# Attention scores in quarter-array matmuls, one stacking transfer for queries and keys, maxima rows from SyncE, and another start, middle and end

## What is computed

```
# attention, 16 heads of width 8
q, k, v = LN(x) @ Wq.T + bq, ctx @ Wk.T + bk, ctx @ Wv.T + bv
x = x + softmax(q k.T / sqrt(8)) v @ Wo.T + bo
# FFN with two gates (so, si) over the 128 channels of every token
x2 = LN(x)
gate = softmax(GELU(BatchNorm(conv(x2))) @ lin_w.T + lin_b)      # BatchNorm over all 8192 tokens
out  = (x2 @ W) * top32(gate_so) + (x2 * top32(gate_si)) @ W + bias
x = x + out
```

## Time and profile before

| | |
|---|---|
| median of 3 runs | 560.53 us (558.9 to 560.83) |
| the profiled execution | 563.33 us |
| its span, first to last instruction | 560.8 us, so 2.5 us lie around it |
| mean granted TensorE clock | 0.737 of full speed |
| busy share | PE 72%, DVE 79%, ACT 67%, POOL 59% |
| stage 1, step t=0 starts | 34.6 us |
| stage 1 ends, stage 2 starts | about 303 us, 311 us |

### The profile page before, as it was taken

The page is one execution under the profiler, slowest core; times in us unless marked ns, Lnnn a source line. Parts: engine busy times, 40 slices in busy tenths (PEclk is TensorE's granted clock), DMA queues, the critical chain, the costliest instruction groups (busy, mean ns, idle before and its releaser), DMA issues.

```text
span 560.8 us, 15570 instructions
## 1 busy us (share of the span) xinstructions
PE 405.9 (72%) x5186; PEld 316.1 (56%) x5186; DVE 440.5 (79%) x2165; ACT 375.1 (67%) x1060; POOL 330.2 (59%) x402
## 2 busy tenths in 40 slices
PE   3467988999998999988992766666666666666432
PEld 1135766777777777777860545545555555445331
DVE  7745666777877777776541799999999999999990
ACT  2425676877788777766655967777677666676652
POOL 6466676887677777562112046666666666666666
PEclk9857999999999999999795555555555555555555
DMA  4888786888887887675000000000000000000000
GB/s 135 177 206 207 193 199 151 194 185 185 192 195 191 206 187 185 161 168 123 4 4 1 0 2 19 19 20 20 19 20 19 20 20 19 20 20 19 19 20 19
DMA packets 138680, 52.78 MB, mean 94 GB/s; under 512 B 105115, under 2 KB 130908, under 8 KB 137052
## 3 DMA queue, kind: packets, MB, share of 16 engines
q1 hardware_dynamic: 136424, 51.27, 37.8%
q10 hardware_dynamic: 2176, 0.52, 0.4%
HBM read 34.47 MB, written 16.78 MB: 91 GB/s over the span
## 4 chain that ended last, share of the span: by engine, by line
DVE 41%; SPq 33%; DMA 9%; PE 7%; issue 5%; POOL 2%; ACT 2%; POOLq 0%; ACTq 0%; DVEq 0%
SPq L273 30%; DVE kst L868 22%; DVE top_next L859 12%; DMA k_scratch<-k_parts 6%; DVE top_first L859 4%; DMA qst<-q_scratch 3%; SPq L258 3%; PE ps_pv L329 1%; PE ps_col L314 1%; POOL kst L963 1%; ACT x2n L550 1%; PE ps_mix L534 1%; PE ps_row L358 1%; PE ps_row L503 1%; SPq L220 1%
## 5 line engine op out<-in xcount | busy, mean ns | idle before, releaser
L738 DVE TENSOR_REDUCE m<-ps_row 128x8 f32<-128x512 f32 x128 | 82.4, 686 | 54.5 <-PE ps_row L358 54.2
L868 DVE MATCH_REPLACE8 kst<-top_next,kst 128x128 f32<-128x128 f32 x384 | 101.2, 282 | 0.0
L545 ACT ACTIVATE pT<-ps_col 128x512 f32<-128x512 f32 x128 | 68.7, 589 | 37.1 <-PE ps_col L314 37.1
L859 DVE MAX8 top_next<-kst 128x8 f32<-128x128 f32 x384 | 78.2, 282 | 0.0
L329 PE MATMUL ps_pv<-vx,pT 128*64 128x18 f32 x2048 | 72.5, 213 | 0.0
L329 PEld LDWEIGHTS ps_pv<-vx,pT 128*64 128x64 f32 x2048 | 66.1, 139 | 6.3 <-issue 4.2
L519 PE MATMUL ps_proj<-wf_sb,x2T 128*128 128x128 f32 x128 | 33.2, 441 | 45.8 <-ACT x2T L682 45.8
L519 PEld LDWEIGHTS ps_proj<-wf_sb,x2T 128*128 128x128 f32 x128 | 28.5, 328 | 52.2 <-ACT x2T L682 52.2
L550 ACT ACTIVATE x2n<-xr,nm,rs 128x128 f32<-128x128 f32 x128 | 52.6, 493 | 4.2 <-POOL nm L888 4.2
L959 POOL TENSOR_SCALAR neg_max<-top_first 128x4 f32<-128x4 f32 x32 | 7.1, 222 | 74.8 <-DVE top_first L859 74.8
L358 PE MATMUL ps_row<-kst,qst 96*64 96x128 bf16 x1024 | 42.3, 226 | 12.1 <-DMA qst<-q_scratch 12.0
(11 more groups left out here) (103 smaller groups left out, 1092.7 us busy)
## 6 DMA issues: line engine op xcount, KB each, us to landing
k_scratch<-k_parts SPq DMA_DIRECT2D x32, 192.0 KB, 3.1
q_scratch<-q_parts SPq DMA_DIRECT2D x32, 192.0 KB, 3.0
kst<-k_scratch SPq DMA_DIRECT2D x32, 192.0 KB
qst<-q_scratch SPq DMA_DIRECT2D x32, 192.0 KB
xr<-in_x_dram SPq DMA_DIRECT2D x16, 256.0 KB, 4.3
cT<-in_ctxT_dram SPq DMA_DIRECT2D x16, 256.0 KB, 3.7
kst<-k_scratch SPq DMA_DIRECT2D x32, 128.0 KB
qst<-q_scratch SPq DMA_DIRECT2D x32, 128.0 KB
```

Source lines behind the costliest of these rows:

```text
L545: act.activation(pT[:, b % PT_RING, :, :], ps_col[b % 2][:, :, :], ACT.Exp, scale=SCALE).then_inc(act_exp, 1)
L738: dve.tensor_reduce(m32[:, b // 4, :, 4 * j:4 * j + 4].rearrange("q a h -> q h a"), ps_row[b % 2][:, :, :, :], AX.X, ALU.max).then_inc(dve ...
L859: ins = dve.max(top[:, n, :], src)
L868: ins = dve.match_replace(picked[s][:, p, cols], top[:, n, :], src, PICKED)
```

## The change

- The two sequences of a pair lie in different halves of the partitions (rows 0 to 49 and 64 to 113), with no zeros. `key_side` and `query_side` make four instructions for every head and `hp`, each 48 or 50 rows by 64 output partitions by 64 streamed columns, one in each quarter of the array. Their number doubles. Each call covers 8 heads and both `ps_row` or `ps_col` banks, so that it waits for both maxima (or exponentials) of the call before.
- PE's order: each query-side block now follows the key-side block at a quarter's start; it stood after the `values` block that closes a quarter.
- Queries and keys share a tensor `stacks`; 6 stacking transfers of both take the place of 12, and the keys' pieces are now 8 KB long, as the queries' were. The maxima rows go out from SP in two transfers per half group (`maxima`), in SP's order between the others.
- POOL starts `split_queries` only when `max_parts(t, 0)` is done.
- The start: no memsets of the stacks, weights fetched by ACT, an activation that loads ACT's table early, the first keys split by DVE, the first and last layer norms partly on DVE. The middle: batch norm coefficients mostly on DVE, GELU ahead of the repeated normalisation. The end: the last round is done gate by gate, and the last group is combined on DVE, with its transposes and products in halves over four PSUM banks.

The diff, cut to its core:

```diff
-STRIDE = 4
-MROWS = 2 * ROWS
-KROWS = MROWS + 4
+
+KROWS = ROWS + 2
...
+    start = a * 64 + {3: 0, 2: 1, 1: 1 + 2 * 2 * DH}[n]
+    return slice(start, start + 2 * (n * DH - 1) + 1, 2)
...
-        qst = [sb(f"qst{s}", [128, HEADS, HALF], BF16) for s in range(STACKS)]
-        kst = [sb(f"kst{s}", [128, HEADS, PAIRS, 2, SEQ], BF16) for s in range(STACKS)]
-        cT = [sb(f"cT{s}", [128, PAIRS, 2 * SEQ]) for s in range(CTX_RING)]
+
+        stacks = [sb(f"stacks{s}", [128, 2, HEADS, HALF], BF16) for s in range(STACKS)]
+        qst = [stacks[s][:, 0, :, :] for s in range(STACKS)]
+        kst = [stacks[s][:, 1, :, :] for s in range(STACKS)]
...
+            def stack(g):
                 s, d = g % 2, slot(g)
-                wait(sp, done[s], WRITES * (g // 2 + 1))
+                wait(sp, k_out[s], WRITES * (g // 2 + 1))
+                wait(sp, q_out[s], WRITES * (g // 2 + 1))
+
+                wait(sp, pe_col, 8 * (g - STACKS + 1))
+                for n in RUNS:
+                    for a in range(2):
+
+                        if n == 1:
+                            src = scratch[s][a, 0:2 * PARTS:2 * PARTS - 1]
+                            src = src.rearrange("k (i h) t -> i k (h t)", h=HEADS)
+                        else:
+                            step = 2 * PARTS - n
+                            src = scratch[s][a, 0:2 * step].rearrange("(k n) (i h) t -> k n i h t", k=2, h=HEADS)[:, 0:n]
+                            src = src.rearrange("k n i h t -> (n i) k (h t)")
+                        sp.dma_start(stacks[d][spread(a, n), :, :, :].rearrange("r k h t -> r k (h t)"), src).then_inc(moved[d], 16)
...
+            def maxima(g, hp):
+                wait(sp, act_mT, 2 * g + hp + 1)
+                wait(sp, pe_col, 8 * (g - STACKS + 1))
                 for a in range(2):
-                    for n in RUNS:
-                        first = PARTS - n if to_keys else 0
-                        src = scratch[s][a, first:first + n].rearrange("n (i h) t -> (n i) (h t)", h=HEADS)
-                        rows = spread(a, n)
-                        dst = (kst[d][rows, :, :, a, :].rearrange("r h p m -> r (h p) m") if to_keys
-                               else qst[d][rows, :, :].rearrange("r h t -> r (h t)"))
-                        if to_keys:
-                            src = src.rearrange("r (x m) -> r x m", m=SEQ)
-                        sp.dma_start(dst, src).then_inc(moved[d], 16)
+                    rows = slice(a * 64 + ROWS, a * 64 + KROWS)
+                    sp.dma_start(qst[slot(g)][rows, :, hp * 128:(hp + 1) * 128],
+                                 mT[a * 2 * HEADS:(a + 1) * 2 * HEADS, hp, :]).then_inc(m_moved[hp][slot(g)], 16)
...
+                if there(t - 1):
+                    maxima(t - 1, 1)
                 if there(t + 1):
-
-                    wait(sp, act_mT, 2 * t)
-                    wait(sp, pe_col, 8 * (t - 1))
-                    stack(t + 1, k_scratch, k_out, k_moved, True)
-                    stack(t + 1, q_scratch, q_out, q_moved, False)
+                    stack(t + 1)
+                if there(t):
+                    maxima(t, 0)
                 if there(t + 2):
-                    write_parts(t + 2, k_parts, k_scratch, k_out, k_moved)
-                    write_parts(t + 2, q_parts, q_scratch, q_out, q_moved)
+                    write_parts(t + 2, k_parts, PARTS, k_out)
+                    write_parts(t + 2, q_parts, 0, q_out)
...
+                wait(pe, act_exp, 8 * g + 4 * hp + 2 * j)
+                for hh in range(HEADS // 2):
+                    h = j * (HEADS // 2) + hh
+                    for pp, a in ((0, 0), (1, 1), (1, 0), (0, 1)):
+                        rows = slice(a * 64, a * 64 + KROWS)
+                        cols = slice((2 * hp + pp) * SEQ, (2 * hp + pp + 1) * SEQ)
+                        mm = pe.matmul(ps_col[a][pp * SEQ:(pp + 1) * SEQ, hh, :], kst[s][rows, h, cols], qst[s][rows, h, cols],
+                                       start=True, stop=True)
+                        if hh == HEADS // 2 - 1 and pp != a:
+
+                            mm.then_inc(pe_col, 1)
...
+            def query_side(g, hp, j):
+                s = slot(g)
+                if hp == 0 and j == 0:
+                    wait(pe, moved[s], STACK * uses(g))
+
+                wait(pe, dve_max, 8 * g + 4 * hp + 2 * j)
+                for hh in range(HEADS // 2):
+                    h = j * (HEADS // 2) + hh
+                    for pp, a in ((0, 0), (1, 1), (1, 0), (0, 1)):
+                        rows = slice(a * 64, a * 64 + ROWS)
+                        cols = slice((2 * hp + pp) * SEQ, (2 * hp + pp + 1) * SEQ)
+                        mm = pe.matmul(ps_row[a][pp * SEQ:(pp + 1) * SEQ, hh, :], qst[s][rows, h, cols], kst[s][rows, h, cols],
+                                       start=True, stop=True)
+                        if hh == HEADS // 2 - 1 and pp != a:
+
+                            mm.then_inc(pe_row, 1)
...
                 if d:
                     key_side(t - 1, 0, 0)
+                if c:
+                    query_side(t, 0, 0)
                 if e:
                     out_proj(t - 2, 0)
                 if q and t > FIRST + 1:
                     keys(t + 2)
-
                 if d:
                     turn_max(t - 1, 1)
                 if e:
                     values(t - 2, 1, 1)
+
+                if d:
+                    key_side(t - 1, 0, 1)
                 if c:
-                    query_side(t, 0)
-                    query_side(t, 1)
-
-                if d:
-                    key_side(t - 1, 0, 1)
+                    query_side(t, 0, 1)
                 if q:
                     queries(t + 2)
                 if f:
                     turn_x2(t - 3)
                 if e:
                     turn_attn(t - 2, 1)
-
                 if d:
                     values(t - 1, 0, 0)
+
+                if d:
+                    key_side(t - 1, 1, 0)
                 if c:
-                    query_side(t, 2)
-                    query_side(t, 3)
-
-                if d:
-                    key_side(t - 1, 1, 0)
+                    query_side(t, 1, 0)
                 if e:
                     out_proj(t - 2, 1)
                 if c:
                     values_in(t)
-
-                if c:
                     turn_max(t, 0)
                 if d:
                     values(t - 1, 0, 1)
-                if c:
-                    query_side(t, 4)
-                    query_side(t, 5)
                 if f:
                     convolve(t - 3)
 
                 if d:
                     key_side(t - 1, 1, 1)
+                if c:
+                    query_side(t, 1, 1)
                 if n:
                     turn_x(t + 3)
                 if d:
                     turn_attn(t - 1, 0)
-
                 if d:
                     values(t - 1, 1, 0)
-                if c:
-                    query_side(t, 6)
-                    query_side(t, 7)
...
-                wait(act, pe_col, 8 * (g - STACKS + 1))
-                wait(act, act_mT, 2 * g + hp + 1)
-                act.dma_start(qst[slot(g)][MROWS:KROWS, :, hp * 128:(hp + 1) * 128],
-                              mT[:, hp, :]).then_inc(m_moved[hp][slot(g)], 16)
...
+            for dst, src in ((wk_sb, wk), (bqk_sb, bqk), (wq_sb, wq)):
+                act.dma_start(dst[:, :], src).then_inc(qk_in, 16)
+
+            act.wait_ge(dve_half, 2)
+            act.activation(nothing[:, 1:2], nothing[:, 0:1], ACT.Identity)
...
-                j = b % 4
-                if j == 0:
-                    wait(dve, dve_m, 2 * (g - 1) + b // 4 + 1)
-                dve.tensor_reduce(m32[:, b // 4, :, 4 * j:4 * j + 4].rearrange("q a h -> q h a"), ps_row[b % 2][:, :, :, :],
+                hp, j, a = b // 4, (b // 2) % 2, b % 2
+                if b % 4 == 0:
+                    wait(dve, dve_m, 2 * (g - 1) + hp + 1)
+                dve.tensor_reduce(m32[:, hp, a, j * (HEADS // 2):(j + 1) * (HEADS // 2)], ps_row[a][:, :, :],
                                   AX.X, ALU.max).then_inc(dve_max, 1)
...
+            def urgent_rstd(g, ag, ve, rs, nm, ready, added, powered, done):
+
+                wait(dve, ready, g + 1)
+                dve.tensor_scalar(ve[:, :], ag[:, :, 1], LN_EPS, None, ALU.add).then_inc(added, 1)
+                wait(dve, powered, 4 * g + 4)
+                dve.scalar_tensor_tensor(nm, ag[:, :, 0], -1.0, rs, ALU.mult, ALU.mult).then_inc(done, 1)
...
-            dve.memset(kst[0][:, :, :, :, :].bitcast(F32).rearrange("r h p a m -> r (h p a m)"), 0.0).then_inc(dve_zero, 1)
...
+            s = (GROUPS - 1) % 2
+            inner, outer = slice(DIM, 2 * DIM), slice(0, DIM)
+            dve.wait_ge(a2_left, GROUPS)
+            dve.tensor_tensor(expd[s][:, :, inner], expd[s][:, :, inner], picked[s][:, :, inner], ALU.subtract).then_inc(d2_last, 1)
+            dve.wait_ge(d2_last, 1)
+            dve.wait_ge(a2_x2, GROUPS)
```

(16 more changed lines are left out.)

295 lines of the change are left out of this document (162 added, 133 removed).

## The result

The changed kernel takes 624.12 us (median of 4 runs, 622.6 to 625.71), the kernel before 559.71 us beside it. The ratio is 1.116, 95% interval 1.110 to 1.122. The forecast had the sign and missed the size: 575, with a range that ended at 607. Times are medians over all executions; the ratios leave out those more than 1.5% above their kernel's fastest, so the kernels of 590.54 and 603.53 us, with one execution left each (575.98 and 594.33), have none.

The account below looks back on a forecast made before the run. SP's stacking transfers bound stage 1 at 15.6 us a step, PE 1.15 us behind, and DVE bounds stage 2. New waits add 30 us, edges save 15: +15, so 575 us, range 552 to 607.

Parts of the forecast that it names:

- SP's round: SP's transfer issue per loop step: from 15.15 us to 11.5, at worst 13.8, so SP stops being the bound.
- The score pair: Key-side plus query-side block on PE: 0.9 us for 64 instructions, 1.1 with changes of form, against 1.02 before.
- The reading that explained two rows with one number: PE score and value blocks: 64-column weight loads set the time, about 58 ns each, 14.5 ns with four side by side.
- The new waits: PE waits for DVE's maxima ahead of the query side: 2.0 us in the second quarter, 1.05 in the fourth.
- The step: One stage 1 loop step: 14.8 + 2.0 + 1.05 = 17.8 us against 15.6, +30 us over 14 steps.
- only streaming counts: Rival for PE's score pairs: 0.47 + 0.2 us a pair, 16.5 us a step, 555 us in all; chance 0.25.
- The clock: Rival: PE's new waits drop its clock to 1.2 GHz, 3.4 us a stretch, 599 to 623 us, put at 605; chance 0.20.
- I cost that at nothing, up to 1 us a step: Maxima transfers on SP, first half's queued behind the stack: no cost, up to 1 us if the fourth quarter gets short.
- the end (-6): After DVE's last replace: gate-by-gate work and halved transposes and products finish near 552, saving 6 us.
- the middle (-2.3): Between the stages: renormalisation behind the first GELU and an early table load on ACT save 2.3 us.
- The start (-7): First query-side block comes at 27.5 instead of 34.61, saving 7 us (4 to 8).
- 2.7 to land: Start: time from the last query stack's issue to the first query-side block, 34.61 - 31.95 = 2.7 us, assumed unchanged.

Follow-up runs that it names:

- 590.54: Changed kernel with DVE's maxima ahead of the normalisations, maxima rows issued by ACT, and twelve stacking transfers in 8 KB packets instead of six; 590.54 us.
- 603.53 us: The 590.54 us kernel with the first half's maxima rows sent sooner, and PE's output product and keys ahead of the first key side; 603.53 us.
- the edges' kernel: The kernel before with only the changed kernel's start, middle and end, its loop, layout and transfers kept; 553.31 us, ratio 0.984.
- the quarter kernels: The changed kernel and the ten follow-ups that keep its score products in quarters of the array; 581.11 to 624.12 us.
- the split one: The kernel before with each score product issued as two of half its streamed columns, 64 instead of 32 a quarter; 570.75 us, ratio 1.022.

## Why the prediction missed, step by step

- **SP's round** (11.5, at worst 13.8) and its leaving the chain: right, with 9.7 us of issue a step and 4.34 of them for the stack instead of 5.
- **The score pair** (0.9 for 64 instructions, 1.1 in all): wrong. It takes 0.67 us. The reading that explained two rows with one number, a shared weight load of 58 ns, fell (it set float32 value products beside bf16 query-side ones); the lower bound, streaming alone, holds: 178.60 - 178.33 = 0.27 us for the 32 key-side instructions, 8 ns each. Doing without the zeros thus does give PE something, 4 x 0.35 us a step. The Trainium skill's load time by columns ("TensorE: Matmul & The Clock Gate", LDWEIGHTS), shared by four as the forecast shared it, gave an estimate of 0.85 us for the 64; the trace, with 0.27 us for 32 and 0.67 for the pair, doesn't agree, and the measurement decides.
- **The new waits** (2.0 and 1.05 us): the place, the releaser and the first size were right (1.88); the second was 0.49, with 0.34 us more spent ahead of the convolution on ACT's copy.
- **The step** (17.8): the only one of the changed kernel with the clock up throughout takes 16.6 (282.0 to 298.6). That is the 16.5 of the rival "only streaming counts", whose sizes were the right ones.
- **The clock** was a rival at 0.20, and it is what happened. This is the step that failed: the sum of the forecast priced the new wait with the clock at 2.4 GHz and had no term for its falls. I set against it that one step in sixteen had fallen before. But the idle time of 1.28 us in the earlier trace rows was itself one of few over a microsecond, and I forecast a longer one in every step. The price of a fall was about right, the number was not: 14 falls instead of seven, with stretches of 3.4 to 20 us, 8 on average, at 0.40 of each (below) make 45 us, where the rival's "in all" had 48. Falls and pauses of issue together take steps from 16.6 to 20.3 us: 14 x 3.7 = 52 us. The kernel before with the new order alone shows wait and clock together: 14 x (18.9 - 15.5) = 48 us.
- **What I had no term for:** pauses of issue, 11.2 us here and up to 29 us once the wait was gone, and maxima rows that land late. "I cost that at nothing, up to 1 us a step" was too low: with the wait gone, they took 1.5 to 3 us at a time.
- **Edges:** the end (-6) right to 0.1 us and the middle (-2.3) nearly, with 5.2 - 3.7 = 1.5 here and 1.7 in the edges' kernel. Alone, middle and end made 553.31 of 561.14, -7.8. The start (-7) failed: -2.5 at the first query side and nothing at the first value product (38.4, before 38.6). The failed term is "2.7 to land": the last of the six transfers was issued at 24.1 and PE went on at 32.09. With twelve transfers, issued to 27.8, it went on at 31.9, so the bytes set this time, not the issue.

The sum in sizes as measured, for the loop: waits and pauses, 50 us of idle PE against 18 before, +32; 113 us at 1.2 GHz instead of 7, at a price of (1.90 - 1.13)/1.90 = 0.40 of each, +43; score pairs -20. That is +55, where 14 steps show 14 x 4.7 = +66. The 11 us that are missing lie in what this rough price leaves out; I did not find them singly. On the kernel before, the runs show what the new order costs by itself. In the changed kernel they show where the time goes, but the causes stand in for each other when one is taken away, so they can't be priced one by one.

Shown: the order alone costs the kernel before 10%; its falls of the clock come behind the new waits; with six merged transfers the longest pause is 3.1 to 4.3 us, with twelve 1.3 to 1.6, and the doubled number of instructions alone brings none; every pause ends behind a packet of instructions. Only argued: that in the quarter kernels instructions come late since six transfers of double size fill the engines' queues at once. Open: why the quarter kernels with twelve transfers still pause for up to 1.6 us while the split one, with as many instructions, does not. They use up the same number of instructions in shorter bursts (64 in 0.67 us), but no run took that apart.

## What to carry to other kernels

When a block is moved on the engine that sets the pace, follow its operands back through the other engines' queues and see whether the producer now stands just ahead of it; a microsecond of new idle time in every step is to be priced with the clock at its lower level, not without. Where a wait is removed, look for what it had covered: here late rows and late instructions stood behind it, and the undisturbed 14.5 us step was never reached for long. An idle time that a profile calls issue is either late instructions or a wait that it could not name; the semaphores in the kernel's text tell which. Edits at the edges and an edit of the loop are worth timing apart: the edges alone made the kernel 1.6% faster, and the loop hid it.
